# A decoder layer on one core: later slices of the long convolutions read from sixteen copies of their filters

## Chip, cores and metric

One core of a Trainium2 chip. The metric is the device time of one execution in microseconds; the time of the kernel before is the median of three runs. Times in the trace count from the start of the span.

## What is computed

A decoder layer on x of 8 x 256 tokens x 256 channels: a gated delta-rule attention with three depthwise causal convolutions of its values, then cross attention, then a mixture of experts, each with a residual and a layer norm. The change touches only the convolutions of v with the filters fir_s, fir_m and fir_l:

```python
FIR_K = (3, 15, 64)
def _dwconv(x, w):
    K = w.shape[1]
    xt = jnp.pad(jnp.transpose(x, (0, 2, 1)), ((0, 0), (0, 0), (K - 1, 0)))
    y = jax.lax.conv_general_dilated(xt, w[:, None, :], (1,), 'VALID', dimension_numbers=('NCH', 'OIH', 'NCH'), feature_group_count=w.shape[0])
    return jnp.transpose(y, (0, 2, 1))
v = jax.nn.silu(_dwconv(hs @ Wv, conv_v))
paths = jnp.stack([_dwconv(v, fir_s).reshape(b, Ln, H, DV), _dwconv(v, fir_m).reshape(b, Ln, H, DV), _dwconv(v, fir_l).reshape(b, Ln, H, DV), delta_path, v.reshape(b, Ln, H, DV)], axis=3)
```

## The kernel before

The first phase, `phase_project_invert_and_fir`, runs the projections for all eight batches, inverts the small triangular matrices on DVE, and makes the three convolutions on PE. The work is written out as one instruction list for each engine; engines meet only at semaphores. `weave(stages, n, before, beside)` sets the order on one engine: at step s, stage k handles batch s - k, and the stages of a step are interleaved piece by piece. `before[s]` runs ahead of step s, `beside[s]` is interleaved with it.

**Projections.** SP's `sp_fetch(b)` loads x of batch b (L359) and rows of the gate's weights (L363). PE's `pe_project(b)` waits for x, turns it (L404), projects it (L418) and sums the weight rows (L433). `pe_normalise(b)`, one step later and interleaved, turns the results (L447, L456) and makes the key products (L466). ACT and DVE stand between these: copies at L480, the four-tap convolution at L534, the diagonal blocks at L568. SP writes tokens to tok_dram (L382), the blocks to a_dram (L387), and the sums to w1s_dram (L372), each of these last with five rows.

**Filters.** At step 2 SP's `sp_filters` writes the turned filters to DRAM as rt_dram[slice, filter, position, channel]: 8 slices of SL = 32 channels, NF = 3 filters, P + BLK = 192 positions (L335, L338).

**Hank tiles.** The convolution is a matmul with a 128 x 64 Hankel-like matrix for each channel and filter, hank[k, f, s, c] = rt_dram[slice, f, s + k, c]. `sp_hank` loads it for a slice with 13 transfers. Each has 16 rows k, one for each of 16 partitions; a row is a contiguous run of up to 64 positions x 32 channels x 4 B = 8 KB, and the next row starts 128 B further on (L701 to L704). So the 16 rows of a transfer overlap in DRAM almost wholly. A slice is 1112 KB.

**Slices.** There are RING = 4 hank tiles for 8 slices. `sp_first_hank` loads slices 0 to 3 beside steps 4 to 7 of the first weave. `sp_late_hank` loads slices 4 to 7 in the next phase's `sp_first` (L854), each once `pe_fir` is through with the slice four before it (signal fir_made); there the 52 transfers are issued in one run. Behind them SP writes the inverses to t_dram (L592) and loads tokens (L932). `pe_fir` (L633) waits for a slice's 13 transfers (hank_in) and makes 64 matmuls at L650; ACT copies the results (L668) and, after slices 3 and 7, sends them to fir_dram (L598). PE goes on to the next phase (L958) when ACT has copied the last slice.

Of the kernel before, what the change touches and what calls it, by code (L numbers as in the profile page):

```python
# [6 lines left out]
F32 = mybir.dt.float32  # L7
# [7 lines left out]
P = 128  # L15
B, T, D = 8, 256, 256
# [6 lines left out]
NCH = P // CH  # L23
TAPS = 4
FIRS = (3, 15, 64)
NF = len(FIRS)
# [3 lines left out]
BLK = 64  # L30
# [202 lines left out]
ROW = 24  # L233

# [7 lines left out]
def phase_project_invert_and_fir(pg, a, env):  # L242
    nc, pe, act, dve, pool, sp = pg.nc, pg.pe, pg.act, pg.dve, pg.pool, pg.sp
    V, S, G = nc.vector, nc.scalar, nc.gpsimd
    s = pg.signals("Project", "weights wpad_zero wpad raw_zero sel_zero sel_made filters_turned filters_copied filters_out xT_turned xT_copied raw_made raw_copied beta_made tanh beta first mac silu "
                   "sums_made sums_copied conv_turned sq v_copied ss rn_step tok kT_turned kT_copied a_made diag win_zero win_made fir_made stage_copied",
                   "x_in rows_in sums_out tok_out diag_out am_in inv_set inv_step turned inv_out")
    with ExitStack() as mem:
# [90 lines left out]

        def pool_hank_zero():  # L340
            for h in env.hank:
                for f in range(NF):
                    pool.in_turn()
                    G.memset(h[:, f].rearrange("k s c -> k (s c)"), 0.0).then_inc(*pool.tick(env.hank_zero))  # L344
# [7 lines left out]
        def sp_late_hank(sl):  # L352
            sp.wait_ge(s.fir_made, PAIRS * (sl - RING + 1))
            interleave([sp_hank(pg, env, sl)])
# [324 lines left out]
        weave([sp_fetch, sp_project, sp_normalise], B, {2: sp_filters}, {4 + sl: sp_first_hank(sl) for sl in range(RING)})  # L679
# [12 lines left out]
def sp_hank(pg, env, sl, at_a_time=HANK_DMAS):  # L692


    nc, rt, begun = pg.nc, env.rt_dram, 0
    for f, count in ((2, 1), (0, 2)):
        n_taps = FIRS[f + count - 1]
        for k in range(0, P, 16):
            s0, s1 = max(0, P - n_taps - k - 15), min(BLK, P - k)
            if s0 < s1:  # L700
                src = bass.AP(tensor=rt.tensor, offset=((sl * NF + f) * (P + BLK) + s0 + k) * SL,  # L701
                              ap=[[SL, 16], [(P + BLK) * SL, count], [1, (s1 - s0) * SL]])
                nc.sync.dma_start(env.hank[sl % RING][k:k + 16, f:f + count, s0:s1, :].rearrange("k f s c -> k f (s c)"),  # L703
                                  src).then_inc(*env.hank_in[sl % RING].up(16))  # L704
                begun += 1
                if begun % at_a_time == 0:
                    yield
# [1929 lines left out]
def decoder_program(nc, a, plan):  # L2637
    with ExitStack() as ctx:
# [11 lines left out]
        env.rt_dram = nc.dram_tensor("rt_dram", [SLICES, NF, P + BLK, SL], F32).ap()  # L2650
        env.fir_out, env.hank_zero, env.hank_in = pg.counter(), pg.counter(), [pg.counter() for _ in range(RING)]
# [57 lines left out]
```

## Time and profile before

| what | value |
|---|---|
| median of 3 runs | 1010.86 us (1010.31 to 1016.79) |
| the profiled execution | 1008.28 us, span 1006.5 us |
| TensorE's mean granted clock | 0.956 of full speed |
| PE busy | 874.1 us, 87% of the span |
| DVE busy | 634.5 us, 63% |
| ACT busy | 434.1 us, 43% |
| POOL busy | 344.5 us, 34% |
| SP's DMA queue, share of 16 engines | 37.9% |

A busy share is a mean over phases with different limits, so the table says little on one stage. The chain of work that ended last, and the timeline of one engine with what ended its idle time, say what a stage waited for.

### The profile page before, as it was taken

The page shows a single profiled execution, that of the slowest core. Times are in us where ns is not written, and L with a number is a line of the kernel's source. Part 1 is how long each engine was busy: PE and PEld are TensorE (multiplying, and loading weights), DVE is VectorE, ACT ScalarE, POOL GpSimd, SP SyncE. Part 2 cuts the span into 40 slices and gives each one's busy share as a digit, 9 for nine tenths or more (in the row PEclk, how much of TensorE's full clock was granted, in tenths as well). Part 3 has the DMA queues.
Part 4 walks back from the last instruction along what each step waited for, and adds up shares of the span by engine and source line. Part 5 has one row for each costly group of instructions (what it writes and reads, how often), then busy time and mean ns, then how long its engine had stood idle before and what let it go on. Part 6 is the DMA issues. An engine that isn't in the chain of part 4 may idle for free.

```text
span 1006.5 us, 18421 instructions
## 1 busy us (share of the span) xinstructions
PE 874.1 (87%) x6859; PEld 652.5 (65%) x6859; DVE 634.5 (63%) x1488; ACT 434.1 (43%) x781; POOL 344.5 (34%) x318
## 2 busy tenths in 40 slices
PE   6788787779888887889889988889997999999995
PEld 5576566557666665768656655555786777777774
DVE  5788889556898899843656777665444343333255
ACT  5577744354554454543134453445431322222221
POOL 9422100113445555521201124223632142222584
PEclk9899988788999998999989999999999999999998
DMA  5689669896433443112796112000403222221421
GB/s 166 182 234 256 200 117 265 265 205 158 112 52 94 98 75 74 53 53 95 287 389 220 43 59 88 25 23 22 142 17 97 50 64 67 60 63 54 149 67 63
DMA packets 145528, 120.83 MB, mean 120 GB/s; under 512 B 90848, under 2 KB 127776, under 8 KB 144544
## 3 DMA queue, kind: packets, MB, share of 16 engines
q1 hardware_dynamic: 141168, 103.98, 37.9%
q0 software_dynamic: 3408, 9.38, 2.5%
q10 hardware_dynamic: 864, 6.29, 1.5%
q8 instruction: 56, 0.92, 0.4%
q14 instruction: 32, 0.26, 0.1%
HBM read 71.33 MB, written 48.29 MB: 119 GB/s over the span
## 4 chain that ended last, share of the span: by engine, by line
PE 57%; DVE 20%; POOL 7%; ACT 6%; issue 5%; DMA 2%; SPq 2%; ACTq 0%; POOLq 0%; DVEq 0%
PE ps L2462 9%; PE ps L1868 6%; PE ps L2477 5%; DVE cross_room L1901 3%; PE ps L2326 3%; DVE room L534 3%; PE ps L1808 3%; PE ps L1304 2%; DVE big L1356 2%; PE ps L1930 2%; POOL hank L344 2%; PE ps L1570 2%; POOL kept L2609 2%; PE ps L2339 2%; SPq L703 2%
## 5 line engine op out<-in xcount | busy, mean ns | idle before, releaser
L1946 ACT ACTIVATE cross_room<-ps 128x1024 f32<-128x1024 f32 x64 | 65.6, 1024 | 100.0 <-PE ps L1872 97.7
L1901 DVE TENSOR_REDUCE cross_room<-ps 128x4 f32<-128x1024 f32 x64 | 78.1, 1224 | 39.4 <-PE ps L1868 38.6
L2462 PE MATMUL ps<-wr,xbT 128*128 x312 | 99.0, 459 | 1.9 <-ACT xbT L2498 1.9
L1868 PE MATMUL ps<-kept,cross_room 32*128 32x256 f32 x512 | 74.5, 413 | 20.8 <-DVE cross_room L1901 19.3
L2551 POOL DMA_INDIRECT y_dram<-yb,dest_row x39 | 37.6, 963 | 134.5 <-DVE dest_row L2527 130.4
L1272 POOL TENSOR_TENSOR st<-st,exponent 128x20 f32<-128x20 f32 x16 | 56.6, 3535 | 67.5 <-DVE st L1247 66.2
L2462 PEld LDWEIGHTS ps<-wr,xbT 128*128 128x128 f32 x312 | 58.8, 189 | 29.5 <-issue 2.6
L1872 PE MATMUL ps<-cross_room,kept 32*128 32x256 f32 x512 | 75.7, 415 | 0.0
L1868 PEld LDWEIGHTS ps<-kept,cross_room 32*128 32x128 f32 x512 | 47.2, 190 | 38.8 <-issue 20.9
L534 DVE SCALAR_TENSOR_TENSOR room<-room 128x256 f32<-128x256 f32 x144 | 58.3, 479 | 14.9 <-ACT room L484 14.9
L2536 DVE TENSOR_TENSOR cross_room<-cross_room,ps 128x352 f32<-128x352 f32 x39 | 20.3, 521 | 58.6 <-PE ps L2462 57.2
L650 PE MATMUL ps<-hank,win 128*32 128x192 f32 x512 | 45.1, 514 | 10.7 <-DMA hank<-rt_dram 5.7
L2542 DVE TENSOR_SCALAR yb<-ps,weight 128x256 f32<-128x256 f32 x39 | 18.9, 484 | 50.5 <-PE ps L2477 50.5
L2506 ACT ACTIVATE cross_room<-ps 128x352 f32<-128x352 f32 x39 | 18.1, 464 | 73.1 <-PE ps L2462 73.1
L650 PEld LDWEIGHTS ps<-hank,win 128*32 128x32 f32 x512 | 34.0, 150 | 20.9 <-DMA hank<-rt_dram 7.1
L1247 DVE TENSOR_REDUCE st<-paths 128x20 f32<-128x1280 f32 x32 | 47.2, 1478 | 0.2
L1872 PEld LDWEIGHTS ps<-cross_room,kept 32*128 32x128 f32 x512 | 45.2, 190 | 1.8 <-issue 1.4
L418 PE MATMUL ps<-room,weights 128*128 128x256 f32 x192 | 44.5, 389 | 2.1 <-ACT room L474 2.1
L418 PEld LDWEIGHTS ps<-room,weights 128*128 128x128 f32 x192 | 36.8, 195 | 7.7 <-DMA room<-in_conv_v 2.5
L2396 POOL TENSOR_TENSOR hTlo<-cross_room,hThi 128x512 fp32r<-128x512 f32 (+1 forms) x24 | 31.2, 1302 | 30.4 <-ACT hThi L2355 28.9
L2326 PE MATMUL ps<-x2Thi,whi 128*128 128x512 f32 (+1 forms) x96 | 38.6, 402 | 0.6 <-issue 0.6
L2326 PE MATMUL ps<-x2Tlo,whi 128*128 128x512 f32 (+1 forms) x96 | 38.0, 396 | 0.0
(349 smaller groups left out, 2247.4 us busy)
## 6 DMA issues: line engine op xcount, KB each, us to landing
xs_dram<-params SPq DMA_DIRECT2D x17, 1040.0 KB, 18.0
room<-in_gW SPq DMA_DIRECT2D x8, 1280.0 KB, 8.0
tok_dram<-room SPq DMA_DIRECT2D x8, 768.0 KB, 4.4
fir_dram<-room ACTq DMA_DIRECT2D x6, 1024.0 KB, 11.9
paths<-fir_dram SPq DMA_DIRECT2D x48, 128.0 KB, 3.8
xb<-xs_dram SPq DMA_DIRECT2D x39, 130.0 KB, 2.3
yr<-y_dram SPq DMA_DIRECT2D x16, 256.0 KB, 3.4
delta_room<-tok_dram SPq DMA_DIRECT2D x4, 768.0 KB, 7.5
```

Of the source, the lines that this page charges most:

```text
L418: m = nc.tensor.matmul(ps[:, 1 + j, c * T:(c + 1) * T], W[j][:, k, c * P:(c + 1) * P], xT[:, k, :], start=(k == 0), stop=(k == KT - 1))
L534: V.scalar_tensor_tensor(out=conv[:, j, c, :], in0=raw[:, j, c, tap:tap + T], scalar=taps[:, j, c, tap:tap + 1], in1=conv[:, j, c, :], op0 ...
L650: m = nc.tensor.matmul(ps[q * CH:(q + 1) * CH, sl % 2 * PAIRS + pair, u * NF * BLK:(u + 1) * NF * BLK], win[:, sl // RING, :, q * CH + in_ ...
L1247: V.tensor_reduce(st[:, t, k], src[:, :, t, :].rearrange("p n (h d) -> p n h d", h=H), AX.X, ALU.add, **kw).then_inc(*s.stat.up())
L1272: G.tensor_tensor(st[:, t, 3].rearrange("p n h -> p (n h)"), st[:, t, 1].rearrange("p n h -> p (n h)"), env.exponent[:, 1, 0:NPATH * H], A ...
L1868: m1 = nc.tensor.matmul(ps[:, c, t * T:(t + 1) * T], strips(qS[b % 3], g, c)[:, t * P:(t + 1) * P], kS(b, g)[c * CH:(c + 1) * CH], start=T ...
L1872: m2 = nc.tensor.matmul(ps[:, c, t * T:(t + 1) * T], kS(b - 1, g)[c * CH:(c + 1) * CH, t * P:(t + 1) * P], strips(qS[(b - 1) % 3], g, c), ...
L1901: V.tensor_reduce(mx[:, :, g, XD + 2 * h * CH:XD + (2 * h + 1) * CH + 1:CH].rearrange("p t c -> p c t"), ps[:, pair(h), :].rearrange("p c ...
L1946: S.activation(pT[g % 2][:, pair(h)].rearrange("p c k t -> p (c k t)"), ps[:, pair(h), :].rearrange("p c n -> p (c n)"), ACT.Exp).then_inc ...
L2326: m = nc.tensor.matmul(ps[0:fn, 2 * par + j, :], w[a_][:, j, k, f0:f0 + fn], env.x2T[b_][:, k, tg * TG:(tg + 1) * TG], start=(k, a_, b_) = ...
L2462: m = nc.tensor.matmul(ps[:, 2 * (j % 2) + half, 0:FF], xbT[j % 2][:, k, :], wr[:, bass.ds(e, 1), k, half, :].rearrange("p e n -> p (e n)" ...
L2477: m = nc.tensor.matmul(ps[:, 5 + j % 2, 0:D], hbT[j % 2][0:fn, n, :], wdr[n][0:fn, bass.ds(e, 1), :].rearrange("p e n -> p (e n)"), start= ...
```

## The change

A new DRAM tensor rt_rows holds sixteen copies of the filters of slices 4 to 7 (positions 48 to 191 of each slice and filter), one copy for each of the 16 rows of a hank transfer. A copy starts 4 x 3 x 192 x 32 + 1024 = 74,752 elements after the one before it, the last 1024 of them unused. SP writes them ahead of step 5 of the weave in `sp_filter_rows`, with four DRAM-to-DRAM transfers, each of four copies x 12 (slice, filter) pairs x 18,432 B. Their source is read with a stride of zero over the four copies. `sp_hank` for slices 4 to 7 reads row r from copy r, at the same place in it as before; slices 0 to 3 still read rt_dram. `sp_late_hank` also waits for the four transfers.

```diff
 ROW = 24
+ROWS, NO_TAPS = 16, P - FIRS[-1] - 16
+ROWS_APART = RING * NF * (P + BLK) * SL + 1024
...
+        def sp_filter_rows():
+
+            copies = env.rt_rows[:, 0:RING * NF * (P + BLK) * SL].rearrange("r (k m) -> r k m", k=RING * NF)
+            sp.wait_ge(s.filters_out, s.filters_out.made)
+            for r in range(0, ROWS, NCH):
+                nc.sync.dma_start(copies[r:r + NCH, :, NO_TAPS * SL:], env.rt_dram[RING:].rearrange("s f n c -> (s f) (n c)")
+                                  [:, NO_TAPS * SL:].unsqueeze(0).broadcast_to([NCH, RING * NF, (P + BLK - NO_TAPS) * SL])
+                                  ).then_inc(*s.rows_out.up(16))
+
...
         def sp_late_hank(sl):
+            sp.wait_ge(s.rows_out, s.rows_out.made)
             sp.wait_ge(s.fir_made, PAIRS * (sl - RING + 1))
             interleave([sp_hank(pg, env, sl)])
...
-        weave([sp_fetch, sp_project, sp_normalise], B, {2: sp_filters}, {4 + sl: sp_first_hank(sl) for sl in range(RING)})
+        weave([sp_fetch, sp_project, sp_normalise], B, {2: sp_filters, 5: sp_filter_rows}, {4 + sl: sp_first_hank(sl) for sl in range(RING)})
...
 def sp_hank(pg, env, sl, at_a_time=HANK_DMAS):
 
 
-    nc, rt, begun = pg.nc, env.rt_dram, 0
+    nc, begun = pg.nc, 0
+    rt, at, apart = (env.rt_dram, sl, SL) if sl < RING else (env.rt_rows, sl - RING, ROWS_APART + SL)
     for f, count in ((2, 1), (0, 2)):
         n_taps = FIRS[f + count - 1]
-        for k in range(0, P, 16):
+        for k in range(0, P, ROWS):
             s0, s1 = max(0, P - n_taps - k - 15), min(BLK, P - k)
             if s0 < s1:
-                src = bass.AP(tensor=rt.tensor, offset=((sl * NF + f) * (P + BLK) + s0 + k) * SL,
-                              ap=[[SL, 16], [(P + BLK) * SL, count], [1, (s1 - s0) * SL]])
-                nc.sync.dma_start(env.hank[sl % RING][k:k + 16, f:f + count, s0:s1, :].rearrange("k f s c -> k f (s c)"),
+                src = bass.AP(tensor=rt.tensor, offset=((at * NF + f) * (P + BLK) + s0 + k) * SL,
+                              ap=[[apart, ROWS], [(P + BLK) * SL, count], [1, (s1 - s0) * SL]])
+                nc.sync.dma_start(env.hank[sl % RING][k:k + ROWS, f:f + count, s0:s1, :].rearrange("k f s c -> k f (s c)"),
                                   src).then_inc(*env.hank_in[sl % RING].up(16))
...
+        env.rt_rows = nc.dram_tensor("rt_rows", [ROWS, ROWS_APART], F32).ap()
```

## Rows read from the trace of the kernel before

**Rows 1.** The page: span, and the chain that ended last by engine and line.
```profile
span 1006.5 us, 18421 instructions
...
PE 57%; DVE 20%; POOL 7%; ACT 6%; issue 5%; DMA 2%; SPq 2%; ACTq 0%; POOLq 0%; DVEq 0%
PE ps L2462 9%; PE ps L1868 6%; PE ps L2477 5%; DVE cross_room L1901 3%; PE ps L2326 3%; DVE room L534 3%; PE ps L1808 3%; PE ps L1304 2%; DVE big L1356 2%; PE ps L1930 2%; POOL hank L344 2%; PE ps L1570 2%; POOL kept L2609 2%; PE ps L2339 2%; SPq L703 2%
```

**Rows 2.** The chain in order of time, 100 to 240 us: start us, us, what.
```profile
134.23 9.96 PE ps L650 x93
...
163.99 0.43 SPq L703
164.47 11.49 DMA hank<-rt_dram
176.00 6.00 PE ps L650 x62
182.02 0.83 ACT room L668
```

**Rows 3.** PE's timeline, 133 to 183 us: start, us, engine, line, tiles [idle before <-releaser].
```profile
134.23 30.09 PE L650 MATMUL ps<-hank,win 128*32 128x192 f32 x352 [2.37 <-DVE room L568]
169.13 5.99 PE L650 MATMUL ps<-hank,win 128*32 128x192 f32 x64 [4.81 <-DMA hank<-rt_dram]
176.00 5.98 PE L650 MATMUL ps<-hank,win 128*32 128x192 f32 x64 [0.88 <-DMA hank<-rt_dram]
```

**Rows 4.** Windows: busy us of each engine, PE clock, DMA share, GB/s.
```profile
137.00:154.00 17.00, 17.00 (x210) 13.72 (x206) 15.59 (x42) 10.82 (x13) 0.00 (x0) 1.00 0.93 136
160.00:168.00 8.00, 4.32 (x49) 3.33 (x41) 7.31 (x21) 3.44 (x4) 0.96 (x1) 0.95 1.01 408
```

**Rows 5.** The chain in order of time, 66 to 96 us.
```profile
66.56 0.59 PE ps L404 x4
...
70.23 0.60 ACT room L480
...
71.47 1.74 DVE room L534 x5
...
80.18 0.59 PE ps L404 x4
...
93.78 0.59 PE ps L404 x4
```

**Rows 6.** The view of line L359, the loads of x.
```profile
L359 SPq DMA_DIRECT2D room<-in_x x8: 424/572/1481, 0.8 to 98.8; - x8
...
DMA to landing us min/median/max: 3.0/3.7/6.8
```

**Rows 7.** SP's timeline, 0 to 240 us.
```profile
69.82 0.47 SPq L387 DMA_DIRECT2D a_dram<-room  x1
70.34 0.58 SPq L359 DMA_DIRECT2D room<-in_x  x1
...
71.48 2.97 SPq L703 DMA_DIRECT2D hank<-rt_dram  x6
77.70 0.35 SPq L382 DMA_DIRECT2D tok_dram<-room  x1
...
137.47 27.43 SPq L703 DMA_DIRECT2D hank<-rt_dram  x52
```

**Rows 8.** The view of rt_dram, then the page's DMA issues.
```profile
L335 SPq DMA_DIRECT2D rt_dram<-room x8: 436/488/1220, 22.3 to 26.7; - x8
...
rt_dram<-room SPq DMA_DIRECT2D x8, 48.0 KB, 1.8
...
w1s_dram<-room SPq DMA_DIRECT2D x16, 10.0 KB
```

**Rows 9.** DMA issues of 0 to 176 us, then of the whole span: KB, us to landing.
```profile
delta_room<-tok_dram SPq DMA_DIRECT2D x1, 768.0 KB, 14.3
...
delta_room<-tok_dram SPq DMA_DIRECT2D x4, 768.0 KB, 7.5
```

More of the change, by code:

```diff
@@ L244, in phase_project_invert_and_fir @@
     V, S, G = nc.vector, nc.scalar, nc.gpsimd
-    s = pg.signals("Project", "weights wpad_zero wpad raw_zero sel_zero sel_made filters_turned filters_copied filters_out xT_turned xT_copied raw_made raw_copied beta_made tanh beta first mac silu "
+    s = pg.signals("Project", "weights wpad_zero wpad raw_zero sel_zero sel_made filters_turned filters_copied filters_out rows_out xT_turned xT_copied raw_made raw_copied beta_made tanh beta first mac silu "
                    "sums_made sums_copied conv_turned sq v_copied ss rn_step tok kT_turned kT_copied a_made diag win_zero win_made fir_made stage_copied",
```

## The prediction

> **What bounds the kernel now.** I read the page first: the span is 1006.5 us and the run that was profiled took 1008.28 us, 0.3% under the median of 1010.86 us. The chain of work that ended last spreads over every phase and no DMA line stands high in it, so the change can only act where the chain meets the filter transfers [rows 1]. Two places matter.
>
> The first is the convolution stage, 134 to 182 us. The chain's pieces there are PE L650, then a run of SP's issues, then 11.49 us of one filter transfer, then PE L650 again [rows 2]. PE's timeline gives the price: the first 352 matmuls take 30.09 us, 85.5 ns each; the last two groups of 64 take 5.99 and 5.98 us (93.5 ns each) and begin after waits of 4.81 and 0.88 us for a hank transfer [rows 3]. The windows say why those are late. From 137 to 154 us, with nearly only sixteen-row hank reads open, the 16 engines are 93% busy but move 136 GB/s, 136/16/0.93 = 9.1 GB/s each while busy. From 160 to 168 us, when fir_dram writes run too, they move 408 GB/s at the same busy share, 25.2 GB/s each [rows 4]. So the overlapping reads run at about a third of the rate of other traffic, and that the late slices are DMA-bound is true. What they cost is only 4.81 + 0.88 = 5.69 us of waiting, plus 2 x 0.5 us of slower matmuls.
>
> The second is the projection loop, 28 to 125 us. The chain there is a ring PE, ACT, DVE, with a period of 13.6 us (L404 begins at 66.56, 80.18 and 93.78 us) and not one piece that is a DMA [rows 5]. It does hang on a transfer: PE's L404 turns x of batch 5 at 80.18 us, and SP issues the load of that x (L359) at 70.34 us. Loads at L359 land after a median of 3.7 us [rows 6], so this one has some 6 us to spare.
>
> **What the change takes away.** The reads of slices 4 to 7 no longer overlap. Nothing else in their 52 transfers changes: same count, sizes and order, and SP's 27.43 us for issuing them stays [rows 7]. A slice is 1112 KB, 69.5 KB an engine, 2.8 us at 25.2 GB/s against 13 issues of about 0.46 us, 6.1 us. SP then sets the pace. The last issue for slice 7, which ends at 164.90 us, would land some 3 us later, before PE wants that slice: 7 x 64 matmuls less the 32 done before 134.23 us are 416, and 134.23 + 416 x 0.0855 = 169.8 us. The gain is bounded by 0 below (the slowness has another cause) and 6.7 us above (both waits and the slower matmuls go). What is late next is PE itself, so nothing is behind it to find. I take 6 us. t_dram (L592) and the token load behind it also land earlier, but at 182 us the chain goes on through ACT's L668 and not through them; I put that at nothing.
>
> **What it adds, and where.** Four DRAM-to-DRAM transfers are issued by SP before step 5 of the first weave. That is after a_dram (L387) at 69.82 us and before the load of x of batch 5, now at 70.34 us [rows 7]. Together they write 16 x 12 rows of 144 x 32 x 4 = 18,432 B: 3.54 MB. The issues cost SP perhaps 4 x 0.49 to 4 x 1.22 us, 2 to 5 us, by the median and the longest of the nearest row, L335 [rows 8]; SP's idle time from 74.45 to 77.70 us covers 3 of them [rows 7]. The bytes are another matter.
>
> Step one: how many engines carry a copy. The slowest dimension of each transfer counts 4 copies. A hank transfer has 16 rows, and such transfers alone keep all 16 engines 93% busy [rows 4], which fits one row of the slowest dimension on each engine. The only SP transfers with fewer rows in it are those of w1s_dram (L372, 5 rows), and they alone have no landing time on the page [rows 8], where a landing is found from sixteen completions. From this I take 4 copies on 4 engines, 3.54 MB / 4 = 885 KB on each. All four transfers use the same four.
>
> The Trainium skill (DMA: Bandwidth & Descriptors, Rules for kernel authors) speaks outright against this edit: it says that an outermost dimension smaller than 16, and a leading zero-stride broadcast by name, holds the whole transfer to that many engines. By it the count is exactly 4; the rows alone would let it be anything from 4 to 16.
>
> Step two: the rate of one engine. The trace has no DRAM-to-DRAM transfer. Bounds: 25.2 GB/s if reading and writing DRAM cost no more than either does now, 35 us for 885 KB; 9.1 GB/s if four engines that read one row together are held back as the sixteen of the hank loads are, 97 us. Between them: every byte now crosses to DRAM twice, and if the 25.2 GB/s is shared by both crossings a copy runs at 12.6 GB/s, 70 us. I take 70 us. Contention as in the hank loads is less likely for four readers: 4 x 25.2 = 101 GB/s is under the 136 GB/s that sixteen got.
>
> The same page (Latency and other measured facts) gives 214 GB/s per direction at full rate for copies between HBM tensors over all engines. As an estimate by that page, 13.4 GB/s an engine and 66 us, 4 us less than my sum; no run here shows it. Its remark that a row pitch padded by 4 KiB restores the rate bears on the spacing of the copies, which has such a pad.
>
> Step three: who waits. The load of x of batch 5 is issued behind the copies on the same queue, and its share on those four engines comes after the 885 KB. That later transfers on a queue wait for earlier ones shows behind the late slices: the token load that SP issues next but one lands after 14.3 us, where such loads have a median of 7.5 us [rows 9]. The copies start at about 72 us and end at 142 us; x lands about 2 us later, 144 us. PE needs it at 80.2 us. Behind L404 on PE's in-order queue stand batch 5's projections and, interleaved, the normalising of batch 4 (L447, L456, L466); ACT, DVE and POOL wait for those; SP stands at tok_dram of batch 4 (L382), with the rest of the first slices' loads and batch 7's fetch behind it. All of it moves by 144 - 80.2 = 64 us. The row load (L363) behind x is 1280 KB, 80 KB an engine, about 3 us, and is wanted 8 us after x. The wait for the copies before slice 4 ends long before it is reached, since the convolutions move too.
>
> Sum: +64 - 6 = +58 us. On the profiled run 1066 us, on the median 1069 us; I say 1067. With a copy rate of 25.2 GB/s: copies end at 107 us, x lands at 109, +29 - 6 = +23, 1031 to 1034 us. With 9.1 GB/s: 169 and 171 us, +91 - 6 = +85, 1093 to 1096 us.
>
> **Rivals.**
> 1. Half rate on four engines, as forecast: 1067 us. Chance 0.44; with no gain at the late slices (rival 4) it is 1073.
> 2. Full rate on four engines, 1032 us. For it: writes to DRAM and reads from it each reach 25 GB/s an engine now [rows 4]. Against: no row shows both in one transfer. 0.30.
> 3. The copies spread over all 16 engines, or their delay doesn't reach x. This is the other side. Over 16 engines the copy takes 9 us at 25.2 GB/s: it ends at 81 us, x lands at 83, a stall of 3 us against 6 gained, 1006 to 1008 us. It decides where the copy takes less than 12 us (72 + 12 + 2 = 80.2 + 6): ten engines at full rate. At 12.6 GB/s it takes 18 us, +12 - 6 = +6, 1015 us. For it: nothing in the rows proves the count of four. Against: the hank pattern and L372's missing landings. 0.12.
> 4. The change doesn't speed the late reads, as their 9.1 GB/s comes from something else than overlap, such as their having one row for an engine. Against: a row is up to 8 KB, and beside fir_dram, whose packets are 8 KB too, the engines reach 25.2 GB/s [rows 4]. +6 us on any case; 0.06 with a time of its own, 1073 us.
> 5. Contended copying, 1095 us: 0.08.
>
> **How the numbers follow.** The likeliest case is 1067 us. Rates between those of rivals 1 and 2 are as possible as the ends, so the range runs from 1028 (rival 2 with a slightly shorter copy) to 1080 us (rival 4 on rival 1); it leaves out rivals 3 and 5, 0.20. A few per mille separate runs here (1010.31 to 1016.79), so about 1% is what a measurement can tell from no change. Slower by over 1%: rivals 1, 2, 4 and 5, 0.88. Rival 3 holds 0.12; most of it is within 1% (0.09), and 0.03 I leave for a gain over 1%, which needs more than the 6.7 us to be had.
>
> **What the profile after would show.** PE idle ahead of L404 of batch 5, released by DMA room<-in_x, by about 64 us (29 with full rate, 3 with sixteen engines), and POOL, ACT and DVE idle there too. A DMA share near 4/16 = 0.25 in that stretch, at 50 GB/s copied by half rate or 100 by full rate. If the share is near 1 instead, rival 3 holds. In the convolution stage no PE wait for hank, seven slices at 85.5 ns a matmul, landings of 2 to 4 us, and GB/s over the late loads set by SP's issues, about 180. If PE still waits there for hank, rival 4 holds. The forecast is wrong at step one if x lands on time with the copies in flight, at step two if the stall is far from 64 us.

## The result: 1045 us against 1011 us, and the profile after

The changed kernel takes 1045.03 us (median of 4 runs, 1035.9 to 1050.27), the kernel before beside it 1011.43 us (median of 4, 1010.31 to 1016.79). The ratio is 1.033 with a 95% interval of 1.0284 to 1.0375, so 33.6 us slower (by the interval, 28.7 to 37.9 us). Medians here and below count every execution, while ratios and their intervals leave out those that took over 1.5% more than the fastest of their kernel. The profiled execution took 1050.27 us, 42 us over the profiled one of before, so its sum is made apart from that of the medians.

PE's timeline after, 76 to 240 us (start, us, engine, line, tiles, and the idle time ahead with its releaser; lines are 12 or 13 higher than before, so L404 is L416, L447 is L459, L650 is L662):

```profile
78.63 1.16 PE L478 MATMUL ps<-room 64*128 64x128 f32 x16 [0.68 <-ACT room L530]
106.92 1.12 PE L416 MATMUL ps<-ident,room 128*128 128x128 f32 x4 [27.13 <-DMA room<-in_x]
...
110.38 5.76 PE L430 MATMUL ps<-room,weights 128*128 128x256 f32 x24
...
121.49 2.08 PE L478 MATMUL ps<-room 64*128 64x128 f32 x16 [0.68 <-ACT room L530]
123.94 1.12 PE L416 MATMUL ps<-ident,room 128*128 128x128 f32 x4 [0.37 <-DMA room<-in_x]
...
140.55 1.12 PE L416 MATMUL ps<-ident,room 128*128 128x128 f32 x4
...
168.09 29.99 PE L662 MATMUL ps<-hank,win 128*32 128x192 f32 x352 [2.65 <-DVE room L580]
201.46 11.74 PE L662 MATMUL ps<-hank,win 128*32 128x192 f32 x128 [3.38 <-DMA hank<-rt_rows]
```

PE stands 27.13 us for the x of batch 5: L416 turns it at 106.92 us instead of 80.18 [rows 5], +26.7. The next two batches take 17.0 and 16.6 us where 13.6 was the period. The large run of convolution matmuls begins at 168.09 us instead of 134.23 [rows 3]: +33.9 at that point. And the late slices do not stop waiting: 3.38 us for a transfer from the new copies.

SP's queue after, the answers to [rows 7]:

```profile
69.85 2.50 SPq L347 DMA_DIRECT2D rt_rows<-rt_dram  x4
72.39 0.50 SPq L371 DMA_DIRECT2D room<-in_x  x1
...
73.45 30.22 SPq L716 DMA_DIRECT2D hank<-rt_dram  x6
...
110.00 5.28 SPq L407 DMA_DIRECT2D room<-a_dram  x3
115.32 0.42 SPq L371 DMA_DIRECT2D room<-in_x  x1
...
171.34 27.45 SPq L716 DMA_DIRECT2D hank<-rt_rows  x52
```

The four copies are issued in 2.50 us, x right behind them at 72.39 us. Six small filter loads behind that, which took SP 2.97 us before [rows 7], now hold it for 30.22 us, so SP can't go on issuing. The windows say what the DMA engines do meanwhile. A row has the window, then the busy us of PE, of its weight loads, of DVE, ACT and POOL, each with a count, then PE's granted clock, the DMA share and GB/s. The second window lies in the late slices' loads:

```profile
82.00:98.00 16.00, 0.00 (x0) 0.00 (x0) 0.00 (x0) 0.00 (x0) 0.00 (x0) 0.56 0.25 106
171.00:188.00 17.00, 17.00 (x209) 12.41 (x205) 15.62 (x41) 11.14 (x13) 0.00 (x0) 0.95 0.93 146
```

From 82 to 98 us no engine computes, the DMA share is exactly 0.25, four engines of sixteen, and 106 GB/s move: 26.5 GB/s on each of the four. The late loads, from copies that no longer overlap, move 146 GB/s at a share of 0.93, 146/16/0.93 = 9.8 GB/s an engine, against 9.1 before [rows 4]: 7% more, where the prediction had 25.2. The page's DMA issues of the copies, and those issued from 71 to 104 us for x (KB of one, us to landing):

```profile
rt_rows<-rt_dram SPq DMA_DIRECT2D x4, 864.0 KB
room<-in_x SPq DMA_DIRECT2D x1, 256.0 KB, 34.5
```

x lands after 34.5 us where 3.7 was the median [rows 6]; 3.54 MB over four engines at 26.5 GB/s is 33.4 us. The copies have no landing time, as those of w1s_dram had none [rows 8].

**Where the further 7.1 us come from.** PE's windows around the two long batches, same columns:

```profile
107.00:111.00 4.00, 4.00 (x18) 3.91 (x19) 0.17 (x1) 1.81 (x3) 0.00 (x0) 0.50 0.91 177
...
124.00:128.00 4.00, 4.00 (x18) 3.91 (x19) 1.45 (x5) 1.79 (x3) 0.00 (x0) 0.50 0.97 283
```

After 27 us of idling the granted clock is 0.50, the lower of the two levels (1.2 GHz), at the start of the batch, and 0.50 again at the start of the next; before, the clock from 66 to 94 us was 1.00. For comparison a batch of before, PE's timeline:

```profile
92.62 1.16 PE L466 MATMUL ps<-room 64*128 64x128 f32 x16 [0.67 <-ACT room L518]
93.71 0.66 PE L404 MATMUL ps<-ident,room 128*128 128x128 f32 x4
...
95.52 5.37 PE L418 MATMUL ps<-room,weights 128*128 128x256 f32 x24
```

From the start of L416 to that of L430 a batch takes 3.46 us at the lower level instead of 1.81, L478 takes 2.08 instead of 1.16, L430 5.76 instead of 5.37: 1.65 + 0.92 + 0.39 = 2.96 us a batch. In the second long batch (16.6 - 13.6 = 3.0) that is all of it. The batch behind it starts slowly too (L430 at 143.00 us, 2.45 us after L416, not 1.81) and gives most of the 0.7 us that are left of the 7.1. In the first (17.0 - 13.6 = 3.4) 0.37 us of waiting for x comes on top, but x is a bound of its own there: SP reaches its load late, behind loads of a_dram that it issues slowly, as the chain of work in order of time has it (start, us, what):

```profile
110.00 4.35 SPq L407
...
115.32 8.57 DMA room<-in_x
```

Had PE run at the upper level there, it would have waited for x instead. Clock and x end within 0.4 us of each other.

The size of this term is one execution's. In e2 below, whose edit comes later in the kernel, the second batch is back at the upper level soon (PE's timeline of e2):

```profile
124.90 1.11 PE L416 MATMUL ps<-ident,room 128*128 128x128 f32 x4
...
139.02 0.66 PE L416 MATMUL ps<-ident,room 128*128 128x128 f32 x4
```

Its first batch takes 16.8 us and its second 14.1, and from L416 of batch 5 to the large run e2 loses 3.7 us and not 7.1. The other traces with a stall, e1, e7 and e8, lose 3.9, 4.0 and 4.4 us there. So the slow first batch shows every time, and a second one slow to its end only in this trace.

**Where the gain of the late slices went.** PE's convolution run from 168.09 to 213.20 us takes 45.1 us, against 47.8 before (134.23 to 181.98 [rows 3]), so PE does save 2.6 us. The next phase needs DVE too. Its timeline before, and then after, at the end of the stage (COPY is the last step of the triangle inversion, L628 before and L640 after; the subtraction behind it is what PE's next phase waits for):

```profile
181.37 1.03 DVE L628 COPY room<-room 128x1024 f32<-128x1024 f32 x1
182.32 0.68 DVE L1066 TENSOR_TENSOR kept<-delta_room,beta 128x512 f32<-128x512 f32 x1
```

```profile
215.28 1.09 DVE L640 COPY room<-room 128x1024 f32<-128x1024 f32 x1
216.30 0.66 DVE L1079 TENSOR_TENSOR kept<-delta_room,beta 128x512 f32<-128x512 f32 x1
```

And PE's timeline after, at the first instruction that waits for it:

```profile
217.02 1.11 PE L971 MATMUL ps<-ident,kept 128*128 128x128 f32 x4 [2.24 <-DVE kept L1079]
```

DVE ends its inversion 33.98 us later than before, while the stage began 33.86 us later. PE's 2.6 us become standing time, 2.24 us of it ahead of L971. The gain is zero, because DVE was already due at the same moment as PE.

So +33.9 at the end of this stage, inside the interval of the medians; that it meets their 33.6 to 0.3 us is luck, as e2 shows how much the term after the stall varies. The profiled pair is 8 us further apart, and that comes later, in stages the change doesn't touch. Windows of 260 to 420 us, before and then after:

```profile
260.00:420.00 160.00, 134.36 (x1302) 101.01 (x1303) 144.07 (x240) 81.40 (x155) 85.97 (x62) 0.96 0.40 85
```

```profile
260.00:420.00 160.00, 143.00 (x1510) 109.58 (x1512) 130.16 (x222) 76.03 (x152) 74.74 (x52) 0.87 0.44 92
```

PE was granted 0.87 there against 0.96. Kernels with no stall at all were granted 0.88, 0.91 and 0.96 in that window (e3, e4 and e12 below), and e4's trace falls behind that of before by about as much over the same stages: at the first matmul of L1808 (L1821 in e4 and after) e4 is 7.0 us late where it was 0.8 us early at the end of the convolution stage, and the changed kernel goes from 33.9 to 42.5 us there. So I take these 8 us as scatter between executions; the profiled one of before was a quick one. No run tested them by themselves.

### The profile page after: what moved, and what is told of

Read it like the earlier page. It is cut to its first block, busy times and chain, and to the rows that moved or that the text cites. A ratio compares the mean times of both kernels' runs of the same rounds, so it can differ in the third digit from the quotient of the medians.

```text
span 1048.5 us, 18426 instructions
## 1 busy us (share of the span) xinstructions
PE 892.6 (85%) x6859; PEld 666.3 (64%) x6859; DVE 632.2 (60%) x1488; ACT 434.0 (41%) x781; POOL 344.8 (33%) x318
## 4 chain that ended last, share of the span: by engine, by line
PE 56%; DVE 21%; POOL 7%; SPq 5%; issue 5%; ACT 4%; DMA 2%; POOLq 0%; DVEq 0%; ACTq 0%
PE ps L2475 9%; PE ps L1881 5%; PE ps L2490 5%; SPq L716 3%; PE ps L1317 3%; DVE cross_room L1914 3%; PE ps L2339 3%; PE ps L1821 3%; DVE room L630 2%; DVE room L633 2%; POOL hank L355 2%; PE ps L1943 2%; PE ps L1583 2%; POOL kept L2622 2%; DVE room L546 2%
## 5 line engine op out<-in xcount | busy, mean ns | idle before, releaser
L1881 PEld LDWEIGHTS ps<-kept,cross_room 32*128 32x128 f32 x512 | 46.7, 188 | 39.7 <-issue 19.1
L662 PE MATMUL ps<-hank,win 128*32 128x192 f32 x512 | 44.8, 513 | 8.7 <-DMA hank<-rt_rows 3.4
L430 PE MATMUL ps<-room,weights 128*128 128x256 f32 x192 | 46.2, 398 | 2.5 <-DMA room<-in_conv_v 2.5
L662 PEld LDWEIGHTS ps<-hank,win 128*32 128x32 f32 x512 | 31.2, 151 | 21.3 <-issue 4.9
L430 PEld LDWEIGHTS ps<-room,weights 128*128 128x128 f32 x192 | 38.2, 203 | 8.6 <-DMA room<-in_conv_v 2.9
L2409 POOL TENSOR_TENSOR hTlo<-cross_room,hThi 128x512 fp32r<-128x512 f32 (+1 forms) x24 | 31.2, 1299 | 30.7 <-ACT hThi L2368 29.2
L590 POOL TENSOR_SCALAR room<-room 128x16 f32<-128x16 f32 x8 | 3.4, 425 | 106.2 <-DVE room L563 106.1
```

Of the source, the lines that this page charges most:

```text
L430: m = nc.tensor.matmul(ps[:, 1 + j, c * T:(c + 1) * T], W[j][:, k, c * P:(c + 1) * P], xT[:, k, :], start=(k == 0), stop=(k == KT - 1))
L662: m = nc.tensor.matmul(ps[q * CH:(q + 1) * CH, sl % 2 * PAIRS + pair, u * NF * BLK:(u + 1) * NF * BLK], win[:, sl // RING, :, q * CH + in_ ...
L1881: m1 = nc.tensor.matmul(ps[:, c, t * T:(t + 1) * T], strips(qS[b % 3], g, c)[:, t * P:(t + 1) * P], kS(b, g)[c * CH:(c + 1) * CH], start=T ...
```

## The experiments

Three questions: is it the four engines that make the stall, is the queue or the engine what x waits in, and what makes the late reads slow.

**e1, the copies over all 16 engines.** Same bytes, same place; the slowest dimension counts 16 copies.

```diff
-            for r in range(0, ROWS, NCH):
-                nc.sync.dma_start(copies[r:r + NCH, :, NO_TAPS * SL:], env.rt_dram[RING:].rearrange("s f n c -> (s f) (n c)")
-                                  [:, NO_TAPS * SL:].unsqueeze(0).broadcast_to([NCH, RING * NF, (P + BLK - NO_TAPS) * SL])
+            for r in range(0, RING * NF, NF):
+                nc.sync.dma_start(copies[:, r:r + NF, NO_TAPS * SL:], env.rt_dram[RING:].rearrange("s f n c -> (s f) (n c)")
+                                  [r:r + NF, NO_TAPS * SL:].unsqueeze(0).broadcast_to([ROWS, NF, (P + BLK - NO_TAPS) * SL])
```

> The changed kernel, but each of the four copying transfers makes all 16 copies of 3 of the 12 (slice, filter) pairs, so that its slowest dimension is 16 and not 4; same bytes, same place. Theory A (the four engines are the loss): a quarter of the load on each engine, 221 KB at the 26.9 GB/s that the packets showed is 8.2 us; copies end near 80 us, x of batch 5 lands near 82, PE waits some 2 us before L416 of batch 5 and not 27, DMA share near 1 while they run; time 1009 to 1014 us. Rival B (the bytes themselves or the extra work on DRAM cost the time, on however many engines): time stays over 1030 us.

Measured: 1021.29 us (10 runs, 1012.91 to 1032.3) against 1008.67, ratio 1.0102 (1.0058 to 1.0146). PE's timeline and the window of the copies in e1:

```profile
85.44 1.12 PE L416 MATMUL ps<-ident,room 128*128 128x128 f32 x4 [7.18 <-DMA room<-in_x]
```

```profile
72.00:82.00 10.00, 4.18 (x35) 2.21 (x34) 8.30 (x21) 4.83 (x11) 0.00 (x0) 0.90 0.98 274
```

The share goes from 0.25 to 0.98 and the stall from 27.13 to 7.18 us, so the count of engines is the cause of the stall. It does not vanish: the engines move 274/16/0.98 = 17.5 GB/s each here, copies and the loads beside them together (19.4 in the same window before, without copies), and a copying transfer lands up to 14.2 us after its issue.

**e2, the copies made and not read.** As the changed kernel, but the late slices read the old tensor.

```diff
-    rt, at, apart = (env.rt_dram, sl, SL) if sl < RING else (env.rt_rows, sl - RING, ROWS_APART + SL)
+    rt, at, apart = (env.rt_dram, sl, SL)
```

> The changed kernel with the copies made and waited for, but slices 4 to 7 read the one array as before. What the new reads give back is then gone. If they give what the profile after suggests (PE waits 3.4 us and not 5.7 for hank), this is 2 to 3 us slower than the changed kernel, 1045 to 1049 us, and the late stage runs at about 9 GB/s an engine as before; if overlap was the cause of the slow reads after all, 6 us slower. If the reads give nothing, no difference.

Measured: 1035.36 us (4 runs, 1030.41 to 1045.23) against 1008.67, ratio 1.0218 (1.016 to 1.0277). PE's timeline of e2 in the late slices:

```profile
200.50 11.45 PE L662 MATMUL ps<-hank,win 128*32 128x192 f32 x128 [4.52 <-DMA hank<-rt_dram]
```

The stall is 27.21 us, as in the changed kernel, and the kernel is not slower than the one that reads the copies, where 2 to 3 us more were expected: reading them is worth nothing, though the wait at the late slices is 1.1 us longer. The interval lies even below that of the change (1.0284 to 1.0375). The traces show 2.2 us of it at the end of the stage: in e2 the term after the stall is 3.4 us shorter and x lands 1.2 us later. The rest is not explained, with four executions of each.

**e3, no copies, sixteen rows onto partitions 8 apart.** Same source rows as in the kernel before, overlapping; only the destination partitions of a late transfer are spread.

```diff
-                nc.sync.dma_start(env.hank[sl % RING][k:k + 16, f:f + count, s0:s1, :].rearrange("k f s c -> k f (s c)"),
+                nc.sync.dma_start(env.hank[sl % RING][(slice(k, k + 16) if sl < RING else slice(k // 16, P, 8)), f:f + count, s0:s1, :].rearrange("k f s c -> k f (s c)"),
```

> The kernel before, but for slices 4 to 7 the 16 rows of a transfer are written to partitions 8 apart (k/16, k/16 + 8, ...) and not to 16 adjacent ones. Sources, sizes, count and order are those of before, so the filters of slices 4 to 7 land in wrong partitions and their results are wrong. Theory C (16 adjacent partitions are the slow place, because few ways into SBUF serve them): the share falls or the rate rises to what SP's issues allow, about 180 GB/s at a share near 0.45, landings of 2 to 4 us, no PE wait for hank, time 1004 to 1007 us. Rival D (overlapping source rows are what is slow) and rival E (one row for an engine is slow in itself): the stage stays at a share of 0.93 and 136 GB/s, PE waits 5.7 us, time as before, 1011 us.

Measured: 1011.71 us (12 runs) against 1008.67, ratio 1.0007 (0.9969 to 1.0045). A window of the late loads, and SP's queue, in e3:

```profile
137.00:154.00 17.00, 17.00 (x210) 12.92 (x206) 15.56 (x42) 9.83 (x12) 0.00 (x0) 1.00 0.51 137
```

```profile
135.27 39.38 SPq L703 DMA_DIRECT2D hank<-rt_dram  x52
```

The same 137 GB/s move at a share of 0.51 instead of 0.93: 16.8 GB/s an engine against 9.1, with sources that still overlap. So the destination made the reads slow. The time doesn't follow, as SP now takes 39.38 us for the 52 issues instead of 27.43 [rows 7] and has become the bound of the loads: PE waits 8.0 us for the last three slices. As in e6 and e9, the filters of slices 4 to 7 lie in the wrong partitions here, so only its times count.

**e6, both: copies over 16 engines, made at step 8 (the edits of e1 above and e4 below), and partitions 8 apart.**

```diff
-                nc.sync.dma_start(env.hank[sl % RING][k:k + ROWS, f:f + count, s0:s1, :].rearrange("k f s c -> k f (s c)"),
+                nc.sync.dma_start(env.hank[sl % RING][(slice(k, k + ROWS) if sl < RING else slice(k // ROWS, P, P // ROWS)), f:f + count, s0:s1, :].rearrange("k f s c -> k f (s c)"),
```

> As e4 (copies over 16 engines ahead of step 8), and slices 4 to 7 also write their rows to partitions 8 apart as e3 did, so that neither source nor destination rows lie close; the filters of slices 4 to 7 land in wrong partitions. Beside e3 it tells what overlapping sources cost once the destination is out of the way. If the overlap costs something of its own, the 6 to 8 KB rows go from e3's 20 GB/s an engine to about 26; if nothing, they stay at 20. SP's slower issues (0.59 us) should stay in both cases, and with them PE's waits.

Measured: 1012.3 us in one run. The same window in e6:

```profile
137.00:154.00 17.00, 17.00 (x208) 13.41 (x204) 15.56 (x43) 10.03 (x12) 0.00 (x0) 1.00 0.54 147
```

147/16/0.54 = 17.0 GB/s an engine without overlap, 16.8 with it (e3). Overlap in the source costs nothing that shows here. With sixteen neighbouring partitions it costs little: 9.1 GB/s an engine before, 9.8 after.

**e9, partitions 2 apart** instead of 8.

```diff
-                nc.sync.dma_start(env.hank[sl % RING][k:k + 16, f:f + count, s0:s1, :].rearrange("k f s c -> k f (s c)"),
+                nc.sync.dma_start(env.hank[sl % RING][(slice(k, k + 16) if sl < RING else slice(k // 32 * 32 + k // 16 % 2, k // 32 * 32 + 32, 2)), f:f + count, s0:s1, :].rearrange("k f s c -> k f (s c)"),
```

> As e3, but the 16 rows of a transfer of slices 4 to 7 go to every second partition of a block of 32 and not 8 apart over all 128 (again the filters of slices 4 to 7 land in wrong partitions). Theory C in the form of the Trainium skill's map (SBUF — State Buffer, Door 1: The DMA port swizzle; partitions fold onto 16 ports in groups of four that repeat after 32): adjacent 4 ports, both 2 apart and 8 apart 8 ports, so this runs as e3 did: share near 0.47 over the first 17 us, 8 KB rows near 20 GB/s an engine. If what counts is the distance, or the number of groups of four partitions without the fold (4, 8, 16), it lies between: share about 0.65, rows near 14 GB/s.

Measured: 1017.41 us in one run; the window in e9:

```profile
137.00:154.00 17.00, 17.00 (x210) 12.47 (x206) 15.59 (x42) 10.61 (x13) 0.00 (x0) 1.00 0.47 124
```

16.5 GB/s an engine, as with 8 apart: both spacings lift the rate from 9.1 by the same factor, 1.8. The Trainium skill (SBUF — State Buffer, Door 1: The DMA port swizzle) has a map that fits: sixteen neighbouring partitions reach 4 of 16 ports, those 2 apart and those 8 apart both reach 8. Three spacings agree with it here. It doesn't give the rates by itself: by the same map the 32 neighbouring partitions of e10 reach 8 ports and the 80 of e5 reach 12, and both ran at 13.5 GB/s an engine. In e10 and e5 the engines were busy all the time and in e3, e6 and e9 half of it, which may be part of the difference; it stays open.

**e5, two wide transfers for a slice** instead of thirteen, on 128 and 80 partitions, still overlapping.

```diff
...
+    for f, count, k in ((2, 1, 0), (0, 2, 48)):
+        src = bass.AP(tensor=rt.tensor, offset=((sl * NF + f) * (P + BLK) + k) * SL,
+                      ap=[[SL, P - k], [(P + BLK) * SL, count], [1, BLK * SL]])
+        nc.sync.dma_start(env.hank[sl % RING][k:P, f:f + count, :, :].rearrange("k f s c -> k f (s c)"),
+                          src).then_inc(*env.hank_in[sl % RING].up(16))
...
```

> The kernel before without copies, but each hank slice is loaded by two transfers, all 128 partitions of the long filter and partitions 48 to 127 of the two short ones, with all 64 positions of a row (the added elements are the zeros that stood there). 2.36 MB a slice and not 1.11, with the source rows overlapping as before; each engine now writes partitions far apart. Theory C (16 adjacent destination partitions are the slow place): over 22 GB/s an engine in spite of the overlap, a slice in about 6 us with no pace set by SP, PE's wait for hank 0 to 2 us, time 4 to 6 us under before. Theory D (overlapping sources are slow): 9 GB/s an engine with twice the bytes, a slice takes 16 us and the late stage grows by some 30 us.

Measured: 1017.58 us (12 runs) against 1006.24, ratio 1.0081 (1.0039 to 1.0122). Two windows of e5, in a load of 128 partitions and in one of 80:

```profile
143.00:146.00 3.00, 3.00 (x43) 2.18 (x37) 2.79 (x7) 1.88 (x3) 0.00 (x0) 1.00 0.97 380
147.00:151.00 4.00, 4.00 (x54) 2.98 (x52) 3.70 (x9) 2.50 (x4) 0.00 (x0) 1.00 1.03 223
```

24.5 GB/s an engine on 128 partitions, 13.5 on 80. The bytes of a slice double, 1024 + 1280 KB instead of 1112, as the rows that are zero are loaded too, and PE waits 4.83 and 4.77 us at the last two slices. The early slices are loaded so too, and there x of a batch comes 1.70 us late.

**e11, e5 from a source without overlap**: rows of gW1, one behind the other, so the filters hold other data and only the times count. The edit against e5:

```diff
-        src = bass.AP(tensor=rt.tensor, offset=((sl * NF + f) * (P + BLK) + k) * SL,
-                      ap=[[SL, P - k], [(P + BLK) * SL, count], [1, BLK * SL]])
+        src = bass.AP(tensor=pg.other.tensor, offset=sl * 131072 + f * P * BLK * SL + k * BLK * SL,
+                      ap=[[BLK * SL, P - k], [P * BLK * SL, count], [1, BLK * SL]])
...
+        pg.other = a["gW1"]
```

> As e5 (two transfers a slice over up to 128 partitions), but the rows come from the gate's weights, each row from 8 KB of its own with no overlap; all filters are then wrong data. It prices the overlap alone with the destination spread as widely as it can be. e5's 8 KB rows ran at 15.6 GB/s an engine. If the overlap costs something of its own they reach 24 to 26 here and PE's two waits of 4.8 us go; if the rate belongs to the destination or to 8 KB rows, they stay near 16.

Measured: 1019.0 us in one run. A window of e11 in a load of 128 partitions:

```profile
145.00:148.00 3.00, 3.00 (x43) 2.12 (x37) 2.79 (x7) 1.88 (x3) 0.00 (x0) 1.00 0.82 339
```

25.8 GB/s an engine against 24.5, and 13.9 (229 GB/s at 1.03) against 13.5 on 80 partitions. A second time, overlap is worth nothing or a few per cent.

**e4, the copies over 16 engines and issued at step 8**, where no x is behind them: the whole idea of the change with its stall taken out.

```diff
-        weave([sp_fetch, sp_project, sp_normalise], B, {2: sp_filters, 5: sp_filter_rows}, {4 + sl: sp_first_hank(sl) for sl in range(RING)})
+        weave([sp_fetch, sp_project, sp_normalise], B, {2: sp_filters, 8: sp_filter_rows}, {4 + sl: sp_first_hank(sl) for sl in range(RING)})
```

> The copies over 16 engines as in e1, and issued ahead of step 8 of the weave, about 111 us, where the profile before shows the DMA engines at a share of 0.2 to 0.5 until 137 us. The copies then cost nothing and what is left is the gain of the separate reads. With the 2.3 us less waiting that the profile after shows: 1008 to 1010 us. If the separate reads are worth the 6 us of my forecast: 1005 us. If the copies still delay something: over 1012 us.

Measured: 1014.07 us (12 runs) against 1008.67, ratio 1.0021 (0.9984 to 1.0058). L416 keeps its steps of 13.6 us. PE's timeline of e4 at the last two slices:

```profile
168.09 5.99 PE L662 MATMUL ps<-hank,win 128*32 128x192 f32 x64 [3.49 <-DMA hank<-rt_rows]
174.81 5.99 PE L662 MATMUL ps<-hank,win 128*32 128x192 f32 x64 [0.73 <-DMA hank<-rt_rows]
```

Waits of 3.49 and 0.73 us against 4.81 and 0.88 [rows 3]. Without the stall the copies neither cost nor give anything that can be measured: the interval runs from 1.6 us quicker to 5.9 us slower.

**e7, the four copies on ACT's queue**, at the same step.

```diff
-            sp.wait_ge(s.filters_out, s.filters_out.made)
+            act.wait_ge(s.filters_out, s.filters_out.made)
             for r in range(0, ROWS, NCH):
-                nc.sync.dma_start(copies[r:r + NCH, :, NO_TAPS * SL:], env.rt_dram[RING:].rearrange("s f n c -> (s f) (n c)")
+                nc.scalar.dma_start(copies[r:r + NCH, :, NO_TAPS * SL:], env.rt_dram[RING:].rearrange("s f n c -> (s f) (n c)")
...
-        weave([idle, act_project, act_normalise], B, {2: act_filters})
+        weave([idle, act_project, act_normalise], B, {2: act_filters, 5: act_filter_rows})
```

> The changed kernel with the same four copying transfers issued from ACT's queue, ahead of ACT's step 5, and not from SP's. Theory A1 (later transfers wait because they stand behind the copies on one queue): SP's x of batch 5 shares the four engines with the copies and lands after some 5 to 15 us and not 34.5; PE waits little for it, the row load (L375) becomes the late one, time 1015 to 1035 us. Rival A2 (an engine finishes what it has, whichever queue it came from): x lands as late as in the changed kernel, 1040 to 1050 us.

Measured: 1047.97 us in one run. PE's and SP's timelines of e7, its DMA issues of 70 to 106 us, and the packets of 93 to 98 us by queue (q10 is ACT's, q1 SP's; packets, MB, share of 16 engines):

```profile
107.55 1.12 PE L416 MATMUL ps<-ident,room 128*128 128x128 f32 x4 [22.79 <-DMA room<-in_x]
```

```profile
71.47 5.12 SPq L371 DMA_DIRECT2D room<-in_x  x1
76.64 10.17 SPq L375 DMA_DIRECT2D room<-in_gW  x1
86.85 18.37 SPq L716 DMA_DIRECT2D hank<-rt_dram  x6
```

```profile
room<-in_x SPq DMA_DIRECT2D x1, 256.0 KB, 36.0
a_dram<-room SPq DMA_DIRECT2D x1, 128.0 KB, 34.7
```

```profile
q10 hardware_dynamic: 32, 0.52, 24.1%
q1 hardware_dynamic: 32, 0.00, 0.5%
```

x has a queue without copies and still lands after 36.0 us, PE turns it at 107.55 us as against 106.92. So another queue doesn't get x past the busy engines. The packets say how. From 93 to 98 us the two queues move 32 packets each, one for one: after each small packet of SP's queue comes one of the copy, 18,432 B, 0.7 us at 26.5 GB/s. Ahead of x in SP's queue stands a_dram, issued at 70.81 us, 128 KB in runs of 128 B, 64 for each engine. By an estimate from these figures 64 turns take 45 us, longer than the copies last, and a_dram indeed lands only 34.7 us after its issue and x 2 us behind it. The Trainium skill (DMA: Bandwidth & Descriptors, Queues, rings and completion order) says that an engine takes turns between queues packet by packet, and this trace agrees. What x would have done with no a_dram ahead of it was not run; its own share is 16 KB an engine.

**e8, the four copies made twice**, the second time into another tensor.

```diff
+            more = env.rt_more[:, 0:RING * NF * (P + BLK) * SL].rearrange("r (k m) -> r k m", k=RING * NF)
+            for r in range(0, ROWS, NCH):
+                nc.sync.dma_start(more[r:r + NCH, :, NO_TAPS * SL:], env.rt_dram[RING:].rearrange("s f n c -> (s f) (n c)")
+                                  [:, NO_TAPS * SL:].unsqueeze(0).broadcast_to([NCH, RING * NF, (P + BLK - NO_TAPS) * SL])
+                                  ).then_inc(*s.rows_out.up(16))
```

> The changed kernel with the four copying transfers made twice, the second time into a tensor that nobody reads: 1.77 MB on each of four engines, 66 to 67 us at 26.9 GB/s. If the stall is the time of the copies on those engines, as the forecast had it, PE waits 27.1 + 33 = 60 us before L416 of batch 5 and the run takes some 33 to 36 us more than the changed kernel, 1078 to 1084 us. If something else held x back (a fixed delay, SP's issue), the wait stays near 27 us.

Measured: 1068.29 us in one run. PE's and SP's timelines of e8:

```profile
140.84 1.12 PE L421 MATMUL ps<-ident,room 128*128 128x128 f32 x4 [59.90 <-DMA room<-in_x]
```

```profile
84.97 10.17 SPq L376 DMA_DIRECT2D room<-in_x  x1
```

The stall grows from 27.1 to 59.9 us: 32.8 us for 885 KB more on each engine, 27 GB/s. SP is held too, 10.17 us for the single issue of x. The time grows by only 18 to 23 us over the changed kernel (1050.27 profiled, 1045.03 median), not by 33. By the start of the large convolution run all of it is there (199.31 against 168.09 us, 31.2); it is later that e8 is quicker than the profiled run after, with a granted clock of 0.92 from 260 to 420 us against 0.87. With one run I leave it at that.

**e10, seven loads of 32 partitions** for a slice, from the kernel before, no copies.

```diff
-        for k in range(0, P, 16):
-            s0, s1 = max(0, P - n_taps - k - 15), min(BLK, P - k)
+        for k in range(0, P, 32):
+            s0, s1 = max(0, P - n_taps - k - 31), min(BLK, P - k)
```

> The kernel before without copies, but every hank slice is loaded by 7 transfers of 32 adjacent rows and not by 13 of 16 (1.60 MB a slice, the added elements are zeros that stood there). By theory C 32 adjacent partitions are served as well as rows 8 apart: 16 to 20 GB/s an engine, a slice in 5 to 6 us and not 7.6, and SP issues 7 and not 13. The four late slices and fir_dram's 7.5 us are through by about 168 us, before PE wants slice 7 at 170 us: no waits at L650 and 4 to 6 us less than before. If overlapping sources set a rate of 9 to 10 GB/s an engine whatever the destination, a slice takes 11 us and this is 10 us slower or more.

Measured: 1009.05 us (12 runs) against 1009.31, ratio 1.001 (0.9971 to 1.0048). A window of the late loads in e10:

```profile
137.00:154.00 17.00, 17.00 (x211) 13.68 (x206) 15.59 (x42) 10.34 (x13) 0.00 (x0) 1.00 1.02 221
```

That is 13.5 GB/s an engine. PE waits once, 2.68 us, and is done with the convolutions after 43.96 us, 3.8 sooner than before; then it stands 3.36 us for DVE's subtraction.

**e12, the long filter in one load of 128 partitions**, the short ones in five of sixteen, no copies: what the findings point to.

```diff
...
+    src = bass.AP(tensor=rt.tensor, offset=(sl * NF + 2) * (P + BLK) * SL, ap=[[SL, P], [(P + BLK) * SL, 1], [1, BLK * SL]])
+    nc.sync.dma_start(env.hank[sl % RING][:, 2:3, :, :].rearrange("k f s c -> k f (s c)"), src).then_inc(*env.hank_in[sl % RING].up(16))
+    yield
-    for f, count in ((2, 1), (0, 2)):
+    for f, count in ((0, 2),):
```

> The kernel before without copies; the long filter of a slice is loaded by one transfer over all 128 partitions (1 MB, overlapping sources as ever) and the two short ones by the five transfers of 16 rows as before (480 KB). Theory C: the wide one runs at 26 GB/s an engine, 2.5 us, as the first transfer of a slice did in e5; the five at 9, 3.5 us; a slice in 6 us and not 8.2, six issues and not 13. Four late slices and fir_dram end some 31.5 us after the first late issue; PE waits 0 to 1 us at L650 and the stretch of L650 ends 5 us sooner after its start than before; in the time 4 to 6 us less, at the edge of what five rounds show. If the overlap sets the rate, the wide one takes 7 us, a slice 10.5, and it is slower by 5 us or more.

Measured: 1008.11 us (12 runs) against 1011.92, ratio 0.9986 (0.9952 to 1.002). PE's timeline of e12, and then DVE's:

```profile
132.11 40.74 PE L650 MATMUL ps<-hank,win 128*32 128x192 f32 x480 [2.40 <-DVE room L568]
...
180.96 1.12 PE L961 MATMUL ps<-ident,kept 128*128 128x128 f32 x4 [6.52 <-DVE kept L1069]
```

```profile
180.22 0.68 DVE L1069 TENSOR_TENSOR kept<-delta_room,beta 128x512 f32<-128x512 f32 x1
```

Both hank waits are gone and PE's run is 40.74 us, 7.0 less: more than the whole gain that was hoped for. All but 0.5 us of it turns into 6.52 us of standing for DVE. The subtraction starts 48.1 us after the run's start, as before (182.32 - 134.23 = 48.1). The times alone would allow 4.9 us of gain (0.9952), the trace does not: the late reads were worth nothing as long as DVE's inversion stands as it does.

Of e3, e5, e10 and e12 a gain of 4 to 7 us was expected each time, and of e4 up to 6; none came. e3 and e5 made PE's waits longer; e10 halved them and e12 took them away, and both met DVE.

## Why the prediction was right, and where its terms were not

The forecast was 1067 us with a range of 1028 to 1080, slower. The median is 1045, inside it, and the direction held. The mechanism was right; two terms of the sum were mis-sized and one was missing, and the errors partly cancel: +64 - 6 = +58 stood for +26.7 + 7.1 + 0, some +34. That the range holds is in part luck: it reached down to rival 2, whose own time, 1032 us, was 13 us too low, and it was wide enough for that.

- **Step one, four copies on four engines, 885 KB on each:** right. The share is 0.25, and e1, which changes only that, cuts the stall from 27.1 to 7.2 us. The rule of the Trainium skill named there (DMA: Bandwidth & Descriptors, Rules for kernel authors) holds.
- **Step two, 12.6 GB/s an engine, 70 us: this step failed.** It gave the 64 us of the sum. A copying engine moves 26.5 GB/s, 33 us; e8's slope, 27 GB/s, says the same. It was reasoned that reading and writing share 25.2 GB/s. That they would not was rival 2, 1032 us, and it is the case that came: it had 29 us of stall, 26.7 were measured. The 25.2 GB/s of a mixed load in [rows 4] was the only row near it, and it held; for the division by two no row spoke. The estimate of 13.4 GB/s from the Trainium skill (DMA: Bandwidth & Descriptors, Latency and other measured facts), a figure for copies over all engines, does not hold for four. With all sixteen copying, e4 has 297 GB/s at a share of 0.97 from 113 to 126 us, 19.1 GB/s an engine, in a window of 3.86 MB of which up to 3.54 are copies. Why that is slower per engine stays open.
- **Step three, x of batch 5 waits behind the copies and all moves with it:** right. The releaser is the x transfer, every engine stands, and x lands at 106.9 us, some 2 us after the copies end by the 33.4 us above. e7 adds that a queue without the copies would not have saved it, as long as a_dram with its small packets stands ahead of x.
- **"All of it moves by" the stall, and no more:** too low by 7.1 us (by 3.7 to 4.4 us in the other four traces with a stall). After the stall PE works at the lower clock level in parts of two batches (3.0 us each), and SP, held by its six issues for 30 us, brings the next x late by about as much. The prediction had the row load behind x at no cost, and never asked in which state the stall leaves the engines and the queue.
- **The gain of 6 us: this term failed twice.** The late reads got only 7% faster, 9.8 GB/s an engine against 9.1; that is rival 4 but for those 7%, and it was given 0.06. Its example of a cause, one row for an engine, is not it: e3 has that too and runs at 16.8. The row used against it was one with fir_dram writes running beside [rows 4]. Those writes leave from 128 partitions, and the mean over both kinds said nothing about loads to sixteen. And "what is late next is PE itself, so nothing is behind it" is wrong: DVE's inversion ended at 182.3 us before, when PE's run did at 182.0. e12 takes both waits away and gains nothing. Its length is in the page's own windows, where DVE is busy 15.59 of 17 us [rows 4].
- **Rival 3, the other side,** would have come true with sixteen engines at a later place (e4, ratio 1.0021), but as "no change": no arrangement tried gave a gain.
- **What I said the profile after would show:** the stall of "29 with full rate" was met within 2 us and the share of 0.25 exactly, at 106 GB/s for 100; the absence of waits for hank was not.

## What to carry to other kernels

Before a big copy is put on a queue, count its slowest dimension: with 4 it took four of sixteen DMA engines here, and what was issued behind it on the same queue was late by the whole copy. Another queue does not help by itself: there each packet waits for one of the copy's, so transfers of many small packets, and what stands behind them, come as late. When a load is slow, look at where it lands before its source: sixteen neighbouring partitions gave 9 to 10 GB/s an engine, 128 gave 25, overlapping rows or not. And a wait is worth what the next engine leaves of it: look up when the other engines finish their part of the stage, on their own timelines, before a gain is written down.

## What was not expected of the hardware

- A DMA engine copies from DRAM to DRAM at 26.5 GB/s when four do so, as fast as any load here; when sixteen do, 19.1, loads beside them included (e4).
- Loads onto 16 neighbouring partitions ran at 9.1 to 9.8 GB/s an engine, onto 16 that are 2 or 8 apart at 16.5 to 17.0, onto 32 neighbouring or 80 at 13.5, onto 128 at 24.5 to 25.8.
- Sixteen strided partitions cost SP more to issue: 39.38 us for 52, 0.76 us each with its pauses, against 27.43, 0.53.
- With four engines clogged, issuing itself stops: 30.22 us for six small loads, 10.17 us for one (e8), on the queue that carries no copies too (18.37 us for six, e7).
- Two queues with work for the same engines moved packet for packet, 32 and 32 in 5 us (e7): 128 B of one for 18,432 B of the other.
- After 27 us without work PE was granted 0.50 of its clock at the start of two batches in a row, with the same short waits between its groups (1.40 and 0.68 us) as the kernel before, which was granted 1.00 through all of them. In e2, with the same stall, it was granted 0.88 from 125 to 129 us, at the start of the second.
